# Second batch's head-output scatters moved out of its attention, 40 scatters in place of 48, and token tiles prepared one tile further ahead

## The reference, cut to what matters

```python
out = jnp.zeros_like(q).at[bi, hi, top_idx].set(out_sel)   # b, h, 307 rows of 16 numbers
x = x + ga * (out.transpose(0, 2, 1, 3).reshape(b, l, D) @ Wo + bo)
```

```python
logits = jnp.einsum('bnd,esd->bnes', xn, sn)      # 2048 x 1024 per batch
dispatch = softmax(logits, axis=tokens); combine = softmax(logits, axis=slots)
slots = jnp.einsum('bnd,bnes->besd', xn, dispatch); out = combine @ experts(slots)
```

## Time and profile before

| what | value |
|---|---|
| median of 3 runs | 1605.75 us (1604.74 to 1607.21) |
| profiled execution, its own time | 1606.21 us |
| its span | 1604.3 us (1.9 us lie around it) |
| granted TensorE clock, mean | 0.989 |
| busy share of the span | PE 92%, DVE 75%, ACT 64%, POOL 17% |
| attention of batch 0, first to last take-out of a head (L1429) | 462.4 to 567.9 us |
| search of batch 1 (L1284) | 573.5 to 870.1 us |
| attention of batch 1, the same | 940.8 to 1058.0 us |
| logits of batch 0, first to last matmul starts (L2051) | 1061 to 1125 us |
| logits of batch 1 | 1342 to 1405 us |

### The profile page before, as it was taken

One profiled execution on the slowest core, in us unless ns is written; L12 is line 12 of the kernel. 1 busy time (PEld: TensorE's weight loads), 2 busy tenths in 40 slices (PEclk: granted clock), 3 DMA queues, 4 the chain that ended last, 5 costly groups with the idle time before them and its releaser, 6 DMA issues.

```text
span 1604.3 us, 28340 instructions
## 1 busy us (share of the span) xinstructions
PE 1470.5 (92%) x8701; PEld 805.9 (50%) x8706; DVE 1203.7 (75%) x2775; ACT 1034.6 (64%) x1418; POOL 270.6 (17%) x328
## 2 busy tenths in 40 slices
PE   7999999998889989999998889989999999989999
PEld 3532222223444422222223634434899886489988
DVE  6579999999887679999999887766855433675511
ACT  4578888887667778888886457743333462334443
POOL 2440000002610051111111213330111000011100
PEclk9999999999999999999999999999999999999999
DMA  5861111122432201112221212220243202024410
GB/s 174 260 166 40 40 42 50 46 55 74 158 90 77 64 21 41 41 41 49 52 56 58 80 32 53 53 78 1 78 150 122 92 30 72 0 64 139 157 50 33
DMA packets 94322, 119.39 MB, mean 74 GB/s; under 512 B 23726, under 2 KB 79630, under 8 KB 93724
## 3 DMA queue, kind: packets, MB, share of 16 engines
q1 hardware_dynamic: 91164, 117.66, 24.5%
q0 software_dynamic: 3072, 0.66, 0.3%
HBM read 93.46 MB, written 24.79 MB: 74 GB/s over the span
## 4 chain that ended last, share of the span: by engine, by line
PE 47%; DVE 32%; issue 13%; ACT 4%; DMA 3%; POOL 1%; DVEq 0%; SPq 0%; ACTq 0%; POOLq 0%
DVE work_area L1284 25%; PE psum L2108 7%; PE psum L2172 7%; PE psum L1966 5%; PE psum L1957 4%; PE psum L2051 4%; PE psum L2119 3%; PE psum L1938 3%; DVE big_area L1284 2%; PE psum L2128 2%; DMA work_area<-heads_out 2%; PE psum L1766 2%; PE psum L2162 2%; PE psum L1791 1%; PE psum L1945 1%
## 5 line engine op out<-in xcount | busy, mean ns | idle before, releaser
L1284 DVE CUSTOM_DVE_ANT_0 work_area<-psum,work_area 128x1024 f32<-128x1024 f32 x512 | 589.4, 1220 | 9.9 <-PE psum L1827 6.3
L885 ACT ACTIVATE work_area<-psum 128x1024 f32<-128x1024 f32 x512 | 510.2, 1026 | 76.7 <-DVE big_area L1284 30.6
L1827 PE MATMUL psum<-work_area 96*128 96x512 bf16 x1024 | 310.8, 385 | 47.7 <-DVE big_area L1284 7.0
L1817 PE MATMUL psum<-work_area 96*128 96x512 bf16 x1024 | 307.2, 382 | 7.4 <-ACT work_area L885 1.9
L1827 PEld LDWEIGHTS psum<-work_area 96*128 96x128 bf16 x1024 | 64.0, 98 | 266.6 <-DVE big_area L1284 242.2
L1817 PEld LDWEIGHTS psum<-work_area 96*128 96x128 bf16 x1024 | 89.3, 98 | 153.9 <-ACT work_area L885 58.1
L907 ACT ACTIVATE work_area<-psum 128x614 f32<-128x614 f32 x160 | 102.2, 682 | 29.1 <-PE psum L1957 25.3
L2172 PE MATMUL psum<-expert_out,work_area 128*128 128x256 f32 x512 | 117.3, 383 | 2.3 <-ACT work_area L1020 2.3
L2108 PE MATMUL psum<-work_area,xn 128*128 128x128 f32 x1024 | 117.2, 275 | 0.0
L2051 PE MATMUL psum<-slots_T,work_area 128*128 128x512 f32 x256 | 115.1, 593 | 1.6 <-ACT work_area L951 1.6
L2108 PEld LDWEIGHTS psum<-work_area,xn 128*128 128x128 f32 x1024 | 115.9, 192 | 0.2
(11 more groups left out here) (263 smaller groups left out, 2052.0 us busy)
## 6 DMA issues: line engine op xcount, KB each, us to landing
work_area<-in_L_ffn_w_dram SPq DMA_DIRECT2D x32, 1024.0 KB, 5.2
work_area<-k_parts SPq DMA_DIRECT2D x192, 64.2 KB
work_area<-q_parts SPq DMA_DIRECT2D x192, 64.0 KB
k_parts<-work_area SPq DMA_DIRECT2D x24, 384.0 KB, 3.5
q_parts<-work_area SPq DMA_DIRECT2D x16, 384.0 KB, 2.7
big_area<-q_parts SPq DMA_DIRECT2D x16, 384.0 KB, 5.9
work_area<-k_parts SPq DMA_DIRECT2D x32, 192.0 KB
x_res<-in_L_attn_x_dram SPq DMA_DIRECT2D x8, 512.0 KB, 6.8
```

The source lines that it names most:

```text
L885: s.activation(SC[:, t % 4], PS[:, 2 * (n % 2):2 * (n % 2) + 2].rearrange("p a n -> p (a n)"), ACT.Relu).then_inc(relu_done, 1)
L1284: v.tensor_tensor_reduce(SC[:, t % 4], PS[:, 4 + 2 * (t % 2):6 + 2 * (t % 2)].rearrange("p a n -> p (a n)"), SC[:, t % 4], 1.0, -3.0e38, A ...
L1817: last = mm(PS[:, 2 * (n % 2) + k], QS1[par][0:TERMS, t * P:(t + 1) * P], KS[par][0:TERMS, k * 512:(k + 1) * 512], start=True, stop=True)
L1827: last = mm(PS[:, 4 + 2 * (t % 2) + k], QS1[par][0:TERMS, t * P:(t + 1) * P], KS[par][0:TERMS, K1 + k * 512:K1 + (k + 1) * 512], start=Tru ...
```

## The change

Batch 1's 48 scatters in its attention are gone. Results and row numbers of all heads of either batch are kept in one place (`ON`, `IDX`, in the old query and key weights). The last chunks of two heads share one transfer: the even head's rests lie on partitions 0 to 63, the odd head's on 64 to 127 (its third chunk begins 64 columns earlier); the 13 unused partitions of each half carry a row number past the real rows. So a batch has 40 scatters. Batch 0's go out in batch 1's search, one per 6 steps. Batch 1's start when 14 of its heads are done (`on_ready` at 30) and go out one after another, the last five when heads 14 and 15 are done. DVE makes the results in two instructions in place of one, and the row numbers too. SP's and ACT's waits for the scatters ahead of the experts' weights and of the first slot maxima are gone; `first_rows(1)` still waits for them all.

In the logits ACT copies the tokens to `XN` (`keep_tokens`) in place of POOL; DVE makes tile t+3 ahead of tile t's maxima; and the last tile is split: DVE takes the maximum of its first 512 columns straight from PSUM while ACT copies the other 512, and PE turns the maxima in two halves. The order of the rest is as it was.

```diff
     k_parts = [nc.dram_tensor(f"k_parts{b}", [3, D, KW], BF16).ap() for b in range(B)]
-    heads_out = [nc.dram_tensor(f"heads_out{b}", [L * H, DH], F32).ap() for b in range(B)]
+    heads_out = [nc.dram_tensor(f"heads_out{b}", [L * H + H, DH], F32).ap() for b in range(B)]
+    UW = 320
+    chunk_at = lambda j, par: j * P - (HALF_ROWS if j == CH - 1 and par else 0)
+    SCATTERS = (2 * PAIRS, 3 * PAIRS)
...
         a = Area(Wqk[:].rearrange("p k c n -> p (k c n)"))
-        ON0 = a.take([H, CH, DH])
-        IDX0 = a.take([H, CH], U32)
+        ON = a.take([H, CH - 1, DH])
+        IDX = a.take([H, CH - 1], U32)
+        ON_ends = a.take([PAIRS, DH])
+        IDX_ends = a.take([PAIRS], U32)
         WoG = sb("Wo_gated", [P, DC, D])
...
-        QS = a.take([2, UP], BF16)
+        QS = a.take([2, UW], BF16)
...
-                    sp.wait_ge(scattered[k], (b + 1) * PAIRS * CH * 16)
+                    sp.wait_ge(scattered[k], (b + 1) * SCATTERS[k] * 16)
                 for t in range(4):
                     head_rows(b, t)
...
-                    sp.wait_ge(scattered[k], B * PAIRS * CH * 16)
...
+                for par in range(2):
+                    g.memset(QS[:, par, U:UW], float(L * H // 2))
                 g.memset(OS[:, U:], 1.0).then_inc(pads_ready, 1)
-            def attend(b):
-
-                def scatter(i, par):
-
-                    pool.wait_ge(on_ready, b * H + i * 2 + (par + 1))
-                    pool.sem_inc(pool_held, 1)
-                    for j in range(CH):
-                        w = min(P, U - j * P)
-                        g.indirect_dma_start(
-                            out=heads_out[b], out_offset=bass.IndirectOffsetOnAxis(ap=IDX[0:w, par, j:j + 1], axis=0),
-                            in_=ON[0:w, par, j], in_offset=None).then_inc(scattered[par], 16)
-
-                with pool.Fori(0, PAIRS) as i:
-                    for par in range(2):
-                        scatter(i, par)
+            def scatter_chunk(b, h, j):
+
+                g.indirect_dma_start(
+                    out=heads_out[b], out_offset=bass.IndirectOffsetOnAxis(ap=IDX[:, h, j:j + 1], axis=0),
+                    in_=ON[:, h, j], in_offset=None).then_inc(scattered[h % 2], 16)
+
+            def scatter_ends(b, i):
+
+                g.indirect_dma_start(
+                    out=heads_out[b], out_offset=bass.IndirectOffsetOnAxis(ap=IDX_ends[:, i:i + 1], axis=0),
+                    in_=ON_ends[:, i], in_offset=None).then_inc(scattered[1], 16)
             def scatter_in_search():
                 pool.wait_ge(zero_out, 64)
+                n = 0
                 for h in range(H):
-                    for j in range(CH):
-                        w = min(P, U - j * P)
-                        pool.wait_ge(max_done, H * NT + 4 + (h * CH + j + 1) * 5)
-                        g.indirect_dma_start(
-                            out=heads_out[0], out_offset=bass.IndirectOffsetOnAxis(ap=IDX0[0:w, h, j:j + 1], axis=0),
-                            in_=ON0[0:w, h, j], in_offset=None).then_inc(scattered[h % 2], 16)
...
+                    for j in range(CH - 1 + h % 2):
+                        n += 1
+                        pool.wait_ge(max_done, H * NT + 4 + n * 6)
+                        if j < CH - 1:
+                            scatter_chunk(0, h, j)
+                        else:
+                            scatter_ends(0, h // 2)
+
+            def scatter_in_logits():
+
+                pool.wait_ge(on_ready, B * H - 2)
+                for h in range(H):
+                    if h >= H - 2:
+                        pool.wait_ge(on_ready, H + h + 1)
+                    for j in range(CH - 1):
+                        scatter_chunk(1, h, j)
+                    if h % 2:
+                        scatter_ends(1, h // 2)
             def experts(b):
-
-                with pool.Fori(0, NT // 2) as i:
-                    for par in range(2):
-                        pool.wait_ge(xs_ready, b * NT + i * 2 + (par + 1))
-                        pool.sem_inc(pool_held, 1)
-                        g.tensor_copy(row(XN, i * 2 + par), XS[:, par]).then_inc(xn_ready, 1)
...
             pads(1)
-            attend(1)
+            scatter_in_logits()
...
+
                 turned(0, 0, 0)
+                keep_tokens(0, 0, 0)
                 with act.Fori(0, NT // 2 - 1) as i:
                     for par in range(2):
                         turned(i, 1 - par, par + 1)
+                        keep_tokens(i, 1 - par, par + 1)
                         keep_logits(i, par)
                 turned(NT // 2 - 1, 1, 1)
+                keep_tokens(NT // 2 - 1, 1, 1)
                 keep_logits(NT // 2 - 1, 0)
                 if b == 0:
                     take_heads(1, 0)
                     take_heads(1, 1)
-                keep_logits(NT // 2 - 1, 1)
+                act.wait_ge(lg_ready, b * NT + NT)
+                s.activation(LS[:, NT - 1, 512:M], PS[:, 5], ACT.Identity).then_inc(lg_half_copied, 1)
+                act.wait_ge(cmax_done, b * (NT + 2) + NT + 1)
+                s.activation(LS[:, NT - 1, 0:512], PS[:, 4], ACT.Identity).then_inc(lg_copied, 1)
                 s.activation(warm[:], onesF[:, 0:1], ACT.Exp)
...
-                for k in range(2):
-                    act.wait_ge(scattered[k], B * PAIRS * CH * 16)
                 slot_maxima(0, 0, S)
                 act.wait_ge(shiftq_ready, b + 1)
...
+                    half = slice(par * HALF_ROWS, (par + 1) * HALF_ROWS)
                     dve.wait_ge(idx_ready, b * H + i * 2 + (n + 1))
-                    if b:
-                        dve.wait_ge(scattered[par], b * (PAIRS * CH * 16) + (i * (CH * 16) + (n // 2) * CH * 16))
-                    v.tensor_scalar(IDX[:, par] if b else of_head(IDX0, i, n), PS[:, 7, CH * P:CH * P + CH], hcol[:, bass.ds(i * 2 + n, 1)], None, ALU.add).then_inc(idx_used, 1)
+                    v.tensor_scalar(of_head(IDX, i, n), PS[:, 7, CH * P:CH * P + CH - 1], hcol[:, bass.ds(i * 2 + n, 1)], None, ALU.add)
+                    v.tensor_scalar(IDX_ends[half, bass.ds(i + n // 2, 1)], PS[half, 7, CH * P + CH - 1:CH * P + CH], hcol[half, bass.ds(i * 2 + n, 1)], None, ALU.add).then_inc(idx_used, 1)
                 def take_out(i, par):
...
-                    v.tensor_tensor(ON[:, par] if b else of_head(ON0, i, n), OR[:, :, 0:DH], ORr.rearrange("p (j o) -> p j o", o=1).to_broadcast([P, CH, DH]), ALU.mult).then_inc(on_ready, 1)
+                    half = slice(par * HALF_ROWS, (par + 1) * HALF_ROWS)
+                    v.tensor_tensor(of_head(ON, i, n), OR[:, 0:CH - 1, 0:DH], ORr[:, 0:CH - 1].rearrange("p (j o) -> p j o", o=1).to_broadcast([P, CH - 1, DH]), ALU.mult)
+                    v.tensor_scalar(ON_ends[half, bass.ds(i + n // 2, 1)].rearrange("p o d -> p (o d)"), OR[half, CH - 1, 0:DH], ORr[half, CH - 1:CH], None, ALU.mult).then_inc(on_ready, 1)
...
+                    for k in range(2):
+                        dve.wait_ge(scattered[k], SCATTERS[k] * 16)
                     spread(0)
...
-                    dve.wait_ge(cmax_done, b * (NT + 1) + i * 2 + (par + 1))
+                    dve.wait_ge(cmax_done, b * (NT + 2) + i * 2 + (par + 1))
                     v.tensor_tensor(CM, CM, tile_of(t), ALU.max).then_inc(cmax_done, 1)
+
+                def last_maximum():
+                    dve.wait_ge(lg_ready, b * NT + NT)
+                    dve.wait_ge(cmax_done, b * (NT + 2) + NT)
+                    v.tensor_tensor(CM[:, 0:512], CM[:, 0:512], PS[:, 4], ALU.max).then_inc(cmax_done, 1)
+                    dve.wait_ge(lg_half_copied, b + 1)
+                    v.tensor_tensor(CM[:, 512:M], CM[:, 512:M], LS[:, NT - 1, 512:M], ALU.max).then_inc(cmax_done, 1)
                 def row_maximum(t):
                     v.tensor_reduce(nrm[:, bass.ds(t, 1)], tile_of(t), AX.X, ALU.max, negate=True)
-                with dve.Fori(0, NT // 2 - 1) as i:
+                def next_tile(i, par, n):
+
+                    dve.wait_ge(xn_ready, b * NT + i * 2 + (n - 1))
+                    dve.wait_ge(xsT_ready, b * NT + i * 2 + (n - 1))
+                    xn_tile(i, par, n)
+
+                next_tile(0, 0, 2)
+                with dve.Fori(0, NT // 2 - 2) as i:
                     for par in range(2):
-
-                        dve.wait_ge(xn_ready, b * NT + i * 2 + (par + 1))
-                        dve.wait_ge(xsT_ready, b * NT + i * 2 + (par + 1))
-                        xn_tile(i, par, par + 2)
+                        next_tile(i, 1 - par, par + 3)
                         slot_maximum(i, par)
                         row_maximum(i * 2 + par)
-                for par in range(2):
-                    slot_maximum(NT // 2 - 1, par)
+                next_tile(NT // 2 - 2, 1, 3)
+                for t in (NT - 4, NT - 3):
+                    slot_maximum(t // 2, t % 2)
+                    row_maximum(t)
+                slot_maximum(NT // 2 - 1, 0)
+                last_maximum()
```

(15 more changed lines are left out.)

8 lines of the change are left out of this document (3 added, 5 removed).

## The result

The changed kernel was slower. Six runs of it gave a median of 1619.71 us (1617.11 to 1621.15), six of the kernel before 1605.3 us (1602.32 to 1607.21): a ratio of 1.0086, with a 95% interval of 1.0075 to 1.0097. The forecast was 1580 us and faster. The profiled execution took 1620.2 us (span 1618.1).

What follows compares the result with a forecast made beforehand. PE bounds attention and logits, so a stage shortens only where PE waits or its partner is late. Gains 11.7 + 6.0 + 5.4 + 2.4 + 0.4 = 25.9 us off 1606.2 gave 1580 us, range 1577 to 1586.

Steps and rivals of the forecast that it cites:

- POOL's new train: Batch 1's 40 transfers, mostly in batch 0's logits, end at 1091.5 with 8 us of cover: cost 0.
- rival 3: Batch 0's logits: DVE's maximum holds POOL's transfers back, head rows 13 us late, 1593 us; chance 0.05.
- Rival 2: Batch 0's logits: the stall moves there with the transfers, 32 x 0.28 = 9 us, 1589 us; chance 0.08.
- Attention, 11.7 us: Batch 1's attention: without scatters beside heads 1 to 14, its whole excess over batch 0's attention is gained, 11.7 us.
- rival 1: Batch 1's attention: ACT's idle time belongs to the batch, not its scatters; 11.7 us not gained, 1592 us; chance 0.14.
- The rule on ports: Batch 1's attention: by this rule ACT's 1.57 us idle isn't the scatter's doing through SBUF; the forecast sided with the profile.
- Logits of batch 1, 5.4 us: Batch 1's logits, tile 0 to tile 14: PE no longer waits for token tiles, 56.5 us become 51.1, gain 5.4 us.
- the end, 2.4 us: After batch 1's last logits: shorter wait for the maximum, 1.7 us, and clock perhaps staying up, 0.7: 2.4 us (1.7 to 3.1).
- Batch 0, 6.0 us: Batch 0's logits, tile 0 to tile 15: PE no longer waits for token tiles, 60.95 us become 54.75 plus 0.2, gain 6.0.

Runs made afterwards that it cites:

- e2: The kernel before without batch 1's 48 transfers (its head results stay zero): 1595.4 us, beside 1595.6 us for the kernel before.
- e10: Changed kernel with batch 1's 40 transfers sent one at a time, spaced out, in its attention and first logits tiles: 1579.0 us, ratio 0.9824 to the kernel before.
- e6: The changed kernel run again, nothing altered: 1583.4 us, ratio 0.9917 to the kernel before at 1596.1 us.
- e5: The kernel before run again, nothing altered, to read its trace: 1594.6 us, beside 1596.1 us in its set.
- e4: Changed kernel with batch 1's 40 transfers sent one at a time, spaced out, in its attention and first logits tiles: 1578.0 us, ratio 0.9885 to the kernel before.
- e13: The changed kernel run again, nothing altered: 1582.2 us, ratio 0.9912 to the kernel before at 1596.3 us.
- e18: The changed kernel run once more, nothing altered: 1582.5 us, ratio 0.9915 to the kernel before at 1595.2 us.
- e7: Changed kernel with batch 1's 40 transfers back in its attention, two or three in a row behind each head: 1578.4 us, ratio 0.9882 to the kernel before.
- e14: Same kernel as e4, in a later set: 1577.9 us, ratio 0.9896 to the kernel before at 1596.3 us.
- e11: Test kernel computing nothing of the block: PE works without a gap, ACT copies, with or without transfers beside; rounds 6.87 us apart without indirect transfers (eight-matmul groups).
- e9: Test kernel computing nothing of the block: two engines hand a tile to each other in nine stages, mostly beside 20 transfers; PE's rounds 1.69 us apart.

## Why the prediction was wrong

- **POOL's new train, "cost 0, until a transfer costs 0.25 us more"**: the step that failed. I looked at one side only, whether POOL would be late, and that part came true to 0.3 us (last transfer from 1090.2 to 1091.2, forecast end 1091.5). In condition A the train cost 40.4 us on the other side, in PE's signals to ACT and DVE. In B it cost 2.2 us (rival 3 below).
- **Rival 2, the stall goes along with the transfers**, had the mechanism and missed the size. Its price, 32 x 0.28 = 9 us, took a mean over groups of three with pauses between and scaled it by their number. With no pause single holds grew to 10 and 20 us: 40.4 us over 40 is 1.0 us each. "ACT has 1.7 us of slack" was no argument against holds of that length.
- **Attention, 11.7 us**: right in condition A (10.6 of it by head 14). In B there is nothing to gain, as e2 shows: 1595.4 without the transfers, 1595.6 with them. That the stall belonged to the transfers was right, and rival 1 is refuted in A by e10. That it belonged to every run of the kernel before was assumed.
- **The rule on ports**: PE and ACT wait on nobody for a port, says the Trainium skill ("SBUF — State Buffer", section Who interferes with whom). No run contradicts it. ACT waited for a signal and not for SBUF; I had set rule and row against each other where both stood.
- **Logits of batch 1, 5.4 us, and the end, 2.4 us**: 51.15 us from tile 0 to tile 14 against a forecast of 51.1. Tile 14 to the slots took 11.84 us both times (1415.25 to 1427.09, and 1376.24 to 1388.08 in e6), before 14.99 (1398.95 to 1413.94): 3.1 us, the upper bound, as the clock stayed up. Batch 0, 6.0 us: in B from tile 0 to tile 15 it is 61.17 us in e5, 57.31 in e6 (3.9 us) and 55.13 in e4, without the train beside it (6.0 us, as forecast). PE's wait for the head rows (1.86 us) is most of what e6 lacks.
- **Rival 3, POOL held by DVE's maximum**: true in B in a smaller size, 0.33 us a transfer over the train in place of 0.67. It ends the cover of 8 us that I had reckoned. From the first logits to the slots e6 takes 67.3 us and e4 65.1, so 2.2 us of the 4 to 5 by which e6, e13 and e18 stand above e4, e7 and e14 are this; the other 2 to 3 are not traced.
- **The number**: 1582 to 1583 us in B lies inside the range by luck, by a sum that does not hold there: the attention term is absent, and the kernel before starts 10 us lower. In A the other terms hold together: e10, with the transfers out of the way, is 27.2 us below its kernel before (1579.0 and 1606.2), where the sum was 25.9. So the train's term is what made the forecast of 1580 us miss by 40.

## What to carry to other kernels

Do not gather indirect transfers into a train because the engine that sends them is free: with the same 40 transfers spread some 2 to 5 us apart, waiting on counts that other engines raise anyway, the kernel took 1578 to 1579 us in both conditions, 0.9824 and 0.9896 of the kernel before, while the train gave 1582 or 1620. All of these times come from recorded runs, so this holds for recorded runs. A stall per transfer, read from short groups with pauses, is not a rate to multiply: 11.7 us over 14 heads, 0.8 us behind a group of three, became single holds of 10 to 20 us beside a train. And where one set's kernel before differs from another's by more than their spread, look for what else differs in the traces (here a missing landing time) before explaining a term.

## What was not expected of the hardware

- The same program ran at 1605 to 1607 us in some sets and at 1595 to 1596 us in others (medians), with no overlap between runs (1602.3 at the lowest, 1600.7 at the highest), and the two are told apart by whether the landings of indirect transfers are in the trace.
- In condition A, 30 indirect transfers 1.26 us apart held PE's signal to ACT for 15.4 us (e11, stage 2: due at 103.2, 6.87 us after 96.29, heard at 118.6), though PE and ACT handed a tile round every 1.69 us beside 20 of them without loss (e9). Transfers without indices held nothing (e11, stage 5). In stage 4 PE's own matmuls came almost to a stand, 15 passes in 23.7 us.
- DVE's work lengthens POOL's indirect transfers: from 0.96 us to 1.7 to 1.9 us beside the maxima in the profile of e6, and to 1.21 to 1.96 us in 4 of 30 beside the maximum alone in stage 7 of e11.
